# An attention and mixture-of-experts kernel on one core: GpSimd's scatters ahead of O_lo, the context's low half on GpSimd, and VectorE's router pieces between its low halves of P

## The reference, cut to what matters

```python
x = x + attention(layernorm(x), ctx)      # x: 64 batches of 128 rows x 128; ctx: 64 x 77 rows x 96
x = x + experts(layernorm(x))

def attention(q_in, ctx):                 # 16 heads of 64
    q = q_in @ w_q; k, v = split(ctx @ w_kv)
    return softmax(q k^T / 8) v @ w_out + b_out

def experts(x):
    logits = x @ router_w.T               # 8 experts, the two with the largest logits per row
    out = sum over the two of logit_e * (silu(x @ w1[e].T) * (x @ w3[e].T)) @ w2[e].T
    return out + (silu(x @ sw1.T) * (x @ sw3.T)) @ sw2.T      # one shared expert
```

## Time and profile before

| | us |
|---|---|
| median of 3 runs (lowest, highest) | 1050.55 (1046.46, 1054.25) |
| the profiled execution | 1049.61 |
| its span, first to last instruction | 1047.7 |
| slots 0 to 63 (to the start of slot 63) | 26.09 to 718.08 |
| mean granted TensorE clock | 0.964 |

### The profile page before, as it was taken

The page is one execution under the profiler, slowest core; times in us unless marked ns, Lnnn a source line. Parts: engine busy times, 40 slices in busy tenths (PEclk is TensorE's granted clock), DMA queues, the critical chain, the costliest instruction groups (busy, mean ns, idle before and its releaser), DMA issues.

```text
span 1047.7 us, 28760 instructions
## 1 busy us (share of the span) xinstructions
PE 948.9 (91%) x9838; PEld 799.4 (76%) x9838; DVE 837.6 (80%) x1904; ACT 647.4 (62%) x1354; POOL 748.1 (71%) x1121
## 2 busy tenths in 40 slices
PE   7899999999999999999999999988699999999910
PEld 6677778788878788778778787866499999987710
DVE  5898989989999998999899999899455556656721
ACT  4676779877777777767777777766234444453300
POOL 5345546767778778767877877887644588888887
PEclk9999999999999999999999999998799999999965
DMA  9154223253342323322434434254346576677421
GB/s 269 47 167 105 51 47 70 46 145 70 62 80 57 82 60 71 70 57 58 82 78 83 79 59 81 60 138 88 75 136 184 156 194 183 169 169 151 141 89 60
DMA packets 222733, 106.55 MB, mean 102 GB/s; under 512 B 160464, under 2 KB 214384, under 8 KB 221456
## 3 DMA queue, kind: packets, MB, share of 16 engines
q1 hardware_dynamic: 214400, 87.91, 35.9%
q0 software_dynamic: 8192, 16.79, 5.9%
HBM read 38.59 MB, written 34.60 MB: 70 GB/s over the span
## 4 chain that ended last, share of the span: by engine, by line
PE 38%; DVE 33%; POOL 13%; issue 9%; ACT 4%; DMA 3%; SPq 0%; DVEq 0%; POOLq 0%; ACTq 0%
POOL ctx_raw L582 9%; DVE top L983 7%; DVE pt_lo L1024 6%; DVE P L993 6%; PE Q L1273 5%; PE W L1137 3%; PE W L1138 3%; POOL ctx_raw L592 3%; PE W L1139 3%; PE S L1205 3%; DVE v_lo L1000 3%; PE W L1381 2%; PE S L1260 2%; PE W L1382 2%; DMA OT_lo<-O_lo 2%
## 5 line engine op out<-in xcount | busy, mean ns | idle before, releaser
L529 POOL TENSOR_TENSOR O_lo<-O,O_hi 128x512 f16<-128x512 f32 x128 | 145.6, 1157 | 162.8 <-ACT O_hi L696 162.8
L1024 DVE TENSOR_TENSOR pt_lo<-Q,pt_hi 77x512 f16<-77x512 f32 x256 | 164.0, 679 | 38.3 <-ACT pt_hi L688 37.5
L478 POOL DMA_INDIRECT xs<-x2cat,pos x128 | 133.0, 1039 | 61.7 <-DMA xs<-x2cat,pos 30.9
L688 ACT ACTIVATE pt_hi<-Q 77x512 f16<-77x512 f32 x256 | 144.4, 589 | 28.0 <-PE Q L1273 27.5
L664 ACT ACTIVATE v_hi<-W,sc 77x512 f16<-77x512 f32 x128 | 87.7, 686 | 117.2 <-PE W L1139 116.4
L1273 PE MATMUL Q<-ident,P 128*77 128x128 f32 x1024 | 148.3, 278 | 2.2 <-ACT P L671 0.8
L582 POOL DMA_INDIRECT ctx_raw<-ys,pos_y x128 | 132.1, 1032 | 23.3 <-issue 21.2
L1205 PE MATMUL S<-G,xTm 128*128 128x462 f32 (+1 forms) x384 | 143.2, 508 | 0.0
L1260 PE MATMUL S<-v_hi,pt_hi 96*128 96x65 f16 x1024 | 109.8, 197 | 28.9 <-DVE P L993 25.9
L1260 PEld LDWEIGHTS S<-v_hi,pt_hi 96*128 96x128 f16 x1024 | 93.9, 97 | 49.5 <-DVE P L993 44.5
L1273 PEld LDWEIGHTS Q<-ident,P 128*77 128x77 f32 x1024 | 122.1, 149 | 3.5 <-issue 2.4
(11 more groups left out here) (256 smaller groups left out, 2902.8 us busy)
## 6 DMA issues: line engine op xcount, KB each, us to landing
ys<-ysb SPq DMA_DIRECT2D x44, 256.0 KB
xg_early<-xs SPq DMA_DIRECT2D x60, 128.0 KB
xp<-x2cat SPq DMA_DIRECT2D x64, 64.0 KB, 1.9
y_out<-X SPq DMA_DIRECT2D x16, 256.0 KB
xg_late<-xs SPq DMA_DIRECT2D x28, 128.0 KB
xs<-zero_in SPq DMA_DIRECT2D x24, 128.0 KB, 2.5
X<-x_in SPq DMA_DIRECT2D x1, 2240.0 KB, 8.2
xs<-x2cat,pos POOLq DMA_INDIRECT x128, 3.0
```

What stands on the lines that cost most here:

```text
L478: pool.indirect_dma_start(out=xs_d[batch_part(b)][:, :], out_offset=index(pos, b, k), in_=x2cat[:, b % RING, :], in_offset=None).then_inc( ...
L529: pool.tensor_tensor(O_lo[:, half_], O[:, (t + 1) % 2, half_], O_hi[:, half_], ALU.subtract).then_inc(s["p_Olo"], 1)
L688: act.activation(pt_hi[0:NK, j % 2, c * 512:(c + 1) * 512], QB[q_bank(j, c)][0:NK, :], ACT.Copy).then_inc(s["a_PThi"], 1)
L1024: dve.tensor_tensor(pt_lo[0:NK, j % 2, c * 512:(c + 1) * 512], QB[q_bank(j, c)][0:NK, :], pt_hi[0:NK, j % 2, c * 512:(c + 1) * 512], ALU.s ...
```

## The change

Four things move. GpSimd's `scatters(t)` stand ahead of `O_low(t)`. `context_low` is GpSimd's, after `O_low` in slots with t % 4 = 3, and TensorE waits for it there (the first one stays on VectorE). VectorE's `choose` and `tables` pieces stand between quarters 0 and 1 of `pt_lo`, and `moments` comes behind quarter 1. The pieces of `tables` skip the slots with t % 8 = 5, 6, 7, 0: part 0 has slots 35, 36, 41 to 44, 49 to 52, 57 and 58, part 1 slots 59, 60 and 65 to 74; part 2 stays. SyncE clears the edges of the experts' regions from two slots after piece 8 on, as before. The pieces of the diff are, in this order, the table of slots, two of GpSimd, three of VectorE and one of TensorE.

```diff
+        TAB_AT = [[t for t in range(first, NB + 4 * CB) if t % CB in (1, 2, 3, 4) or t > NB][:TAB_PIECES] for first in TAB_SLOT]
...
+            def context_low(t):
+                pool.wait_ge(s["a_cg"], (t + 8) // GB)
+                pool.tensor_tensor(cg_lo[:, :], ctx_raw[:, (t + 4) * NK:(t + 4 + GB) * NK], cg_hi[:, :].bitcast(F),
+                                   ALU.subtract).then_inc(s["p_cg"], 1)
...
+                scatters(t)
                 if on(t, 1, NB + 1):
                     O_low(t)
-                scatters(t)
+                if on(t + 1, 0, NB - GB) and t % GB == GB - 1:
+                    context_low(t + 1)
...
                 if on(t, 0, NB):
-                    pt_low(0); pt_low(1)
-                if on(t, -2, NB + 3):
-                    moments(t)
+                    pt_low(0)
                 for piece_ in range(4):
                     if chunk_of(t, S_CHOOSE + piece_) is not None:
                         choose(chunk_of(t, S_CHOOSE + piece_), piece_)
+                for p in range(NP):
+                    if t in TAB_AT[p]:
+                        tables(p, TAB_AT[p].index(t))
+                if on(t, 0, NB):
+                    pt_low(1)
+                if on(t, -2, NB + 3):
+                    moments(t)
...
-                if on(t + 1, FIRST, NB - GB) and j == GB - 1:
-                    context_low(t + 1)
...
-                for p in range(NP):
-                    if on(t - TAB_SLOT[p], 0, TAB_PIECES):
-                        tables(p, t - TAB_SLOT[p])
...
-                        wait(pe, "d_cg", (t + 8) // GB)
+                        pe.wait_ge(s["d_cg"], 1)
+                        wait(pe, "p_cg", t // GB + 1)
```

More of the change, by code:

```diff
@@ L202, in program @@
                  "p_ve p_rstd p_xb p_xln p_x2f p_x2lo p_lg p_M p_pos p_step p_Olo "
-                 "d_pick p_base p_gate "
+                 "d_pick p_base p_gate p_cg "
                  "f_T e_T f_C f_A f_B f_y e_hC e_hA e_X e_add g_sC g_sA g_y "
@@ L213, in program @@
         TAB_PIECES = 12
-        TAIL = max(NB + S_SCATTER, TAB_SLOT[-1] + TAB_PIECES)
+        TAB_AT = [[t for t in range(first, NB + 4 * CB) if t % CB in (1, 2, 3, 4) or t > NB][:TAB_PIECES] for first in TAB_SLOT]
+        TAIL = max(NB + S_SCATTER, TAB_AT[-1][-1] + 1)
         ORDER = list(range(P_START[-1] * CB // GB, NS)) + list(range(P_START[-1] * CB // GB))
@@ L342, in clear_edges @@
                 for p in range(NP):
-                    i = t - TAB_SLOT[p] - TAB_PIECES + 2
+                    i = t - TAB_AT[p][8] - 2
                     if not on(i, 0, EDGE_SLOTS):
@@ L777, in _, with first_context_low @@
         def _(dve):
[L778 to L781, removed]
+            def first_context_low():
+                dve.wait_ge(s["a_cg"], 1)
+                dve.tensor_tensor(cg_lo[:, :], ctx_raw[:, 0:GB * NK], cg_hi[:, :].bitcast(F), ALU.subtract).then_inc(s["d_cg"], 1)
             def largest_of(k):
@@ L799, in _ @@
                 if q == 1:
-                    context_low(FIRST)
+                    first_context_low()
                 if q == 2:
@@ L938, in tables @@
                     dve.wait_ge(s["p_pos"], c + 1)
+                    wait(dve, "d_posy", p)
                     step(dve.tensor_tensor(cnt, base[:, c + 1, :], k[:, K_CAP:K_CAP + E], ALU.subtract))
```

## The result

The changed kernel takes **1072.17 us** (median; 1069.65 to 1073.77), the kernel before in the same comparison 1049.0: ratio **1.0198**, 95% interval 1.0165 to 1.0230: slower, by about 2%. The prediction was 1057, with a range of 1030 to 1067: outside. The profiled execution took 1069.65 us, its span is 1067.8.

What follows compares the result with a forecast made beforehand. VectorE was taken to bound slots with an extra step. Context -4.0, choice +7.2, tables 0 and stage end +2.9 made +6.1; with +1 for the clock, +7 on 1049.61 us, and the median 0.9 higher: 1057 us, range 1030 to 1067.

Steps and rivals of the forecast that it cites:

- the term that decides: Choice pieces between quarters 0 and 1 of pt_lo: the port wait moves to where TensorE waits, +7.2 us over six groups.
- L896 ends 0.08 us after that: Slot 53, choice's second instruction to next slot's start: waits for O_lo's first half, then handoffs; slot 11.42 us, 10.80 before.
- The end of the stage: Slots 60 to 63, without G: O_lo starts earlier and can catch both instructions of a choice piece, +2.9 us.
- The context's low half: Leaves VectorE for GpSimd in 15 places; slots such as 51 shorten, -4.0 us.
- Tables and clock: Table pieces in new slots: about 0, from -2 to +2 us; half-speed clock stretches: +1 us.
- The +1 for more such stretches: TensorE idles about 1 us more in 24 slots, making half-speed clock stretches a little likelier: +1 us.
- Cost and gain 0: GpSimd's scatters ahead of O_lo: O_lo still starts on O_hi, and nobody waits for the scatters inside the stage.
- the middle case: One choice instruction per piece waits for O_lo; 1048 to 1066 us by the bounds of tables, clock and L919, 66%.
- the rival in which both instructions are caught: Choice's first instruction asks for the port after O_lo starts, so both wait: around 1085 us, 10%.
- The case called between: L919 slips in after L901, both table races are won, the clock stays up: 1046 us; partial cases 9%.

Runs made afterwards that it cites:

- experiment 1: The changed kernel with the choice pieces back at their old place behind moments: 1048.21 us, ratio 0.9961 to the kernel before.
- experiment 2: The changed kernel with GpSimd's O_lo held back until VectorE's choice or table piece is done: 1037.84 us, ratio 0.9853 to the kernel before; repeated later 0.9878.
- experiment 4: The kernel before with VectorE's edits alone (choice and tables moved): 1078.29 us, ratio 1.0246.
- experiment 3: The kernel before with GpSimd's edits alone (scatters ahead of O_lo, context's low half on GpSimd): 1053.11 us, ratio 1.0019.
- experiment 8: Changed kernel, O_lo held: one scatter ahead, one behind 0.9887; both ahead of xln 1.0056; both behind, with ScalarE's cg_hi later, 0.9922 (ratios to the kernel before).
- the slower surroundings: Groups of runs where the kernel before takes 1063 to 1071 us, against 1050 in the others.
- experiment 7: Third chip, ratios to the kernel before: changed kernel 1.0256; with O_lo held 1.0136; held, scatters behind 0.9916; kernel before with scatters alone ahead 1.0306.

## Why the prediction was wrong

**The place of the loss: right.** The choice between quarters 0 and 1 was called the term that decides; L902 was to run at 0.22 (0.23), L903 near 1.0 (1.07), TensorE to idle about 1 us per slot (1.07), the wait to be `pt_lo` (35.9 us). Experiments 1, 2 and 4 confirm the mechanism by taking it away and by having it alone.

**Its size: the step that failed.** Slots 53 to 55 take 11.62, not 11.42, and the fourth 11.44, not 11.3. The step "L896 ends 0.08 us after that, quarter 1 runs from 617.18 to 617.86, TensorE starts the transposes at 617.93, and the next slot starts 2.72 later" was short at each link. Quarter 1 starts 8.03 us from the slot's start, not 7.95: the first half of `O_lo` finds L902 at the port and takes 1.22 us, not 1.14 (1.16 in slots without a piece). From the end of quarter 1 to TensorE's start it is not 0.07 us, a handoff that I had taken from ScalarE and GpSimd, but 625.36 - (624.53 + 0.69) = 0.14. From there to the next slot it is 2.76. So 0.2 a slot and 0.75 a group: six groups came to +11.5 for +7.2.

**The end of the stage: the larger miss.** I had +2.9 for slots 60 to 63; slots 60 to 62 alone cost 3.2 and slot 63 another 2.8 (16.9 - 14.1), since in slots 61 to 63 `O_lo` starts 0.4 us ahead of the first two-input instruction and catches both (the timeline of slot 61 above). I had put a price on that but taken it in two slots, at +1 each; the three cost +1.6, +1.0 and +2.8. And behind it I had nothing: from the first expert turn to GpSimd's last scatter the changed kernel takes 97.5 us for 94.6, and since the gathers stand behind the last scatter, this goes into the time whole. In the other kernels of the first group (experiments 1 to 4) the stretch is 94.8 to 97.3 with no order in it, so 3 us is about its scatter, and its cause stays open.

**The context's low half.** -4.0 was foretold, 2.8 of it in slots 3, 7, 11, 19, 27 and 51. These gave 1.7. Slot 51 takes 10.59, not the plain 10.35: once VectorE's half is gone, ScalarE's `cg_hi`, 0.45 us ahead of quarter 2 of `pt_hi`, is late next. With that one moved (experiment 8), these slots fall by another 0.22.

**Tables and clock.** The tables' own items add up to about +1, not 0. Measured, their twelve slots make +0.2, within the bounds and with `cg_lo` gone from two of them, though not slot by slot: slot 43, taken at +0.4 of gain, takes 11.52 for 10.99 because `O_lo` starts at 6.69 there and the second instruction of the piece waits (1.03 us). Slots 37 to 40 lost the half-speed stretch as assumed: the granted clock is 1.00 there, for 0.96. The +1 for more such stretches did not come in the attention: TensorE idles 1 us more in each choice slot, and the clock stays at 1.00 in all windows above but the last.

**The sum.** The span grew by 20.1 us, 14.0 more than the 6.1 of the terms without the clock. By their sizes these are: the choice 4.3, slots 60 to 63 3.1, the stretch to the last scatter 2.9, context and tables together 2.5 (-1.5 for -4.0), slot 5 1.5.

**The scatters ahead at no cost: wrong in general, right where it was measured.** "Cost and gain 0" holds to 0.01 us in plain slots on the first chip. In the groups with the slower surroundings it is a cost as large as the whole change: 1.0275 and 1.0306 alone, 1.0256 with all four edits. No row of the trace of before shows it: its scatters are written from 9.1 in a slot on, and no quarter of `pt_hi` is late there. With the choice at its old place (experiments 1 and 3) it also moved the low half of x2 against L903, +0.12 in slots 53 and 54.

**The range.** The measured time, 1072, lies between the middle case and the rival in which both instructions are caught, and it is a mixture of the two: one caught in slots 13 to 56, both in 61 to 63. The bounds took the tables' and the clock's uncertainty and not that of the working itself: a price of 0.6 us per slot, built from handoffs of 0.07, comes back 24 times. The case called between, put at 1046, adds up to 1050 from its own terms.

## What to carry to other kernels

Filling an engine's idle time with small steps pays only if they don't meet, on a shared port, a long instruction of its neighbour: look at what starts just before or after them. Where they did meet here, one wait that lets the short one go first was worth more than any reordering tried, 34 us of 1072 (experiment 2). And where an edit moves transfers that an engine writes itself over another's critical handoff, time it in more than one place: the fastest kernel of the first group (scatters ahead, held, 0.985) was slower than the kernel before in another (1.014), while the order with one scatter ahead and one behind, or both behind, stays faster in such surroundings (0.989, 0.992).

## What the runs showed of the hardware

- A VectorE `tensor_tensor` of 128x64 with both inputs in SBUF takes 0.23 us alone or beside a scatter, and up to 1.13 beside a GpSimd `tensor_tensor`: it ends 0.08 us after the GpSimd instruction that it found running, and gets in between two that stand back to back. Where it starts 0.02 us ahead of GpSimd's instead, that one takes 1.22 us for 1.16. Getting in between costs the second nothing when the VectorE instruction is 0.23 us long by itself (1.15 for 1.15), and 0.18 us when it is 0.41 long (1.33 in slot 42). The Trainium skill, "SBUF — State Buffer", section "SBUF: two separate sides", has the lock; the traces here agree (1.13 for 0.23 us). A short GpSimd instruction holds as a long one does: 0.35 us beside the 0.42 of x2's low half.
- GpSimd's `tensor_tensor` takes 0.45 us for 128 columns of 32 bits (`xb`), 0.83 for 308 (`cg_lo`), and 1.15 for 512 with a 16-bit output (`O_lo`).
- With two scatters written 0.3 us apart, signals of TensorE to ScalarE and VectorE came up to 1.8 us late in three groups of runs (1.44 in the middle for the second quarters of experiment 7), and on time in the others, with the pair at 2.98 and 2.85 us in slot 22. A single scatter held up none of 56. In the same three groups signals come up to 1.5 us late while gathers 0.6 us apart are written, and in the others none does.
